# Attention with float32r query and key parts in two row tiles in place of bfloat16 parts in column strips

## What is computed

```
q, k, v = x @ Wq.T, x @ Wk.T, x @ Wv.T        # 32 heads of 16; rope on q and k
scores = q @ k.T / 4 + bias[head, i - j]      # bias only where 0 <= i - j < 256
scores = where(i >= j, scores, -inf)
m = max(max_j scores, offset[head])
p = exp(scores - m); out = p @ v / (sum p + exp(offset - m)); y = out @ Wo.T
```

## Time and profile before

| what | value |
|---|---|
| median of 3 runs | 1722.41 us (1719.87 to 1722.74) |
| the profiled execution | 1717.11 us, span 1714.8 us |
| mean granted clock of PE | 0.949 of 2.4 GHz |
| busy in the span | PE 1549.6, PE weight loads 772.6, DVE 1261.3, ACT 866.5, POOL 226.5 us |
| instructions of PE | 22192 products and as many weight loads |
| stack pieces | 192 DMAs of 128.0 KB for each stack |

### The profile page before, as it was taken

One profiled execution on the slowest core, in us unless ns is written; L12 is line 12 of the kernel. 1 busy time (PEld: TensorE's weight loads), 2 busy tenths in 40 slices (PEclk: granted clock), 3 DMA queues, 4 the chain that ended last, 5 costly groups with the idle time before them and its releaser, 6 DMA issues.

```text
span 1714.8 us, 59791 instructions
## 1 busy us (share of the span) xinstructions
PE 1549.6 (90%) x22192; PEld 772.6 (45%) x22192; DVE 1261.3 (74%) x3801; ACT 866.5 (51%) x1148; POOL 226.5 (13%) x102
## 2 busy tenths in 40 slices
PE   7999999938999998999999899899999999788873
PEld 3444444402554555555545454455455454344331
DVE  2444444468887888888788788788788883489996
ACT  2333333211665665566565566566566668444442
POOL 4333333330000000000000000000000000044543
PEclk9999999955999999999999999999899999999995
DMA  5444444772353353263263255244344402112221
GB/s 212 153 147 147 150 156 164 131 176 36 77 90 62 74 100 54 60 113 62 54 118 64 54 98 81 56 80 79 68 76 80 79 24 95 36 48 88 73 74 49
DMA packets 127099, 155.90 MB, mean 91 GB/s; under 512 B 18240, under 2 KB 82880, under 8 KB 126560
## 3 DMA queue, kind: packets, MB, share of 16 engines
q1 hardware_dynamic: 126816, 152.12, 37.4%
HBM read 100.78 MB, written 50.50 MB: 88 GB/s over the span
## 4 chain that ended last, share of the span: by engine, by line
PE 55%; DVE 20%; issue 18%; POOL 3%; DMA 2%; ACT 1%; DVEq 1%; SPq 0%; POOLq 0%; ACTq 0%
PE ps L636 14%; PE ps L703 10%; PE ps L682 10%; PE ps L662 10%; PE ps L688 6%; DVE junk L1141 6%; DVE mx L1134 4%; PE ps L795 2%; POOL probs L1016 2%; PE ps L713 1%; DVE mx L1141 1%; POOL probs L1052 1%; DVE stats L1317 1%; DMA attn<-wvT 1%; DVE work L1249 1%
## 5 line engine op out<-in xcount | busy, mean ns | idle before, releaser
L881 ACT ACTIVATE probs<-ps 128x1024 f32<-128x1024 f32 (+3 forms) x768 | 604.3, 812 | 375.1 <-PE ps L688 341.3
L1141 DVE CUSTOM_DVE_ANT_0 junk<-ps,bias_q 128x384 bf16<-128x384 f32 (+2 forms) x1024 | 500.3, 502 | 112.4 <-PE ps L662 93.2
L662 PE MATMUL ps<-k_stack,q_stack 96*32 96x384 bf16 (+3 forms) x6144 | 519.4, 341 | 52.5 <-DVE mx L1141 30.2
L682 PE MATMUL ps<-q_stack,k_stack 99*32 99x512 bf16 (+3 forms) x6144 | 514.2, 333 | 9.6 <-issue 7.2
L1134 DVE TENSOR_REDUCE mx<-ps 128x1 f32<-128x128 f32 (+3 forms) x768 | 362.1, 485 | 30.0 <-PE ps L662 25.1
L688 PE MATMUL ps<-toep,flip 96*32 96x384 bf16 (+2 forms) x5120 | 370.8, 284 | 4.5 <-issue 4.4
L636 PE MATMUL ps<-attn 128*128 128x512 f32 x768 | 332.6, 596 | 10.4 <-DMA attn<-hT 9.7
L703 PE MATMUL ps<-probs,v_sb 128*32 128x512 f32 (+3 forms) x3072 | 319.1, 489 | 0.1
L662 PEld LDWEIGHTS ps<-k_stack,q_stack 96*32 96x32 bf16 x6144 | 168.4, 97 | 292.3 <-DVE mx L1141 105.2
L636 PEld LDWEIGHTS ps<-attn 128*128 128x128 f32 x768 | 146.7, 191 | 195.5 <-issue 195.5
L682 PEld LDWEIGHTS ps<-q_stack,k_stack 99*32 99x32 bf16 x6144 | 167.3, 96 | 137.8 <-issue 68.6
(11 more groups left out here) (88 smaller groups left out, 957.3 us busy)
## 6 DMA issues: line engine op xcount, KB each, us to landing
q_stack<-q_parts SPq DMA_DIRECT2D x192, 128.0 KB, 4.0
k_stack<-k_parts SPq DMA_DIRECT2D x192, 128.0 KB, 4.1
v_dram<-v_sb SPq DMA_DIRECT2D x32, 512.0 KB, 2.7
v_sb<-v_dram SPq DMA_DIRECT2D x128, 128.0 KB, 3.8
q_parts<-q_stack SPq DMA_DIRECT2D x96, 128.0 KB, 1.9
k_parts<-k_stack SPq DMA_DIRECT2D x96, 128.0 KB, 2.0
attn<-hT SPq DMA_DIRECT2D x8, 1024.0 KB, 6.2
q_stack<-h SPq DMA_DIRECT2D x16, 512.0 KB, 3.9
```

The lines of the kernel that those rows point to most:

```text
L662: mm = pe.matmul(ps_ring[STRIP * a:STRIP * (a + 1), use.bank, 0:c1 - c0], q_stack[0:STACK, b, hl, i:i + STRIP], k_stack[0:STACK, b, hl, c0 ...
L682: mm = pe.matmul(ps_s[STRIP * a:STRIP * (a + 1), u % 2, hh, 0:w], k_stack[0:ROWS, b, hl, j:j + STRIP], q_stack[0:ROWS, b, hl, i0:i0 + w], ...
L881: act.activation(probs[:, (u // 2) % 3, 2 * pr:2 * pr + 2, 0:w], ps_s[:, pr, :, 0:w], ACT.Exp).then_inc(exp_done, 1)
L1141: ins = dve.tensor_tensor_reduce(out=junk[:, use.bank, 0:c1 - lo], in0=ps_ring[:, use.bank, lo - c0:c1 - c0], in1=bias_q[:, hl, BAND - t0 ...
```

## The change

Query and key are kept in two float32r parts (a 4-byte type that is rounded for PE) instead of three bfloat16 parts. Three pieces of 16 rows make 48, and two shift rows 50. Heads 0 and 1 of the group stand in partitions 0 to 49, heads 2 and 3 in 64 to 113, so two heads' products use two row tiles of 64 rows and all 128 columns of the array. A score unit is two products instead of eight, a maxima unit one instead of four, ordered so that neighbours use different row tiles. The bias of all four heads now follows the second unit of a tile, ahead of PV. The maxima are spread over 24 units. Phase 1 has one ACT copy and one DVE subtraction less for each pair, the shift split two DVE steps less. The store of parts is 4 DMAs of 256 KB for each pair instead of 6 of 128 KB; a stack still has 12 pieces. The ones of slots 2 and 3 come by DMA instead of a memset.

```diff
-STACK = 6 * D
-ROWS = STACK + PARTS
+QK_PARTS = 2
+TERMS = 3
+STACK = TERMS * D
+ROWS = STACK + QK_PARTS
+ROW_TILES = 2
+ROW_TILE = P // ROW_TILES
+PAIR = HG // ROW_TILES
-Q_PART = (0, 0, 0, 1, 1, 2)
-K_PART = (0, 1, 2, 0, 1, 0)
-PIECES = 2 * len(Q_PART)
+Q_PART = (0, 0, 1)
+K_PART = (0, 1, 0)
+PIECES = 2 * TERMS * ROW_TILES
+def max_of(k):
+    pair, rest = divmod(k, NMU * ROW_TILES)
+    unit, e = divmod(rest, ROW_TILES)
+    return e, pair, e * PAIR + pair, unit
-SPREAD = 22
+SPREAD = 24
...
 def load_piece(g, b, buf, i):
-                r = i // 2
+                r, e = divmod(i // 2, ROW_TILES)
-                sp.dma_start(dst[D * r:D * (r + 1), buf, :, :],
-                             src[part[r], :, bass.ds(g * HG, HG), b * S:(b + 1) * S])\
+                p0 = ROW_TILE * e + D * r
+                sp.dma_start(dst[p0:p0 + D, buf, :, :].bitcast(FP32),
+                             src[part[r], :, bass.ds(g * HG + e * PAIR, PAIR), b * S:(b + 1) * S])\
...
-                        if i % 3 == 2 and b == 1 and not last:
-                            hl = i // 3
-                            wait_then_address(ring_read, Use(g, b, (hl + 1) * NMU - 1, last).before + 1)
-                            load_bias_q(g + 1, hl)
+                    for pair in range(PAIR) if b == 1 and not last else ():
+                        wait_then_address(ring_read, Use(g, b, (pair + 1) * NMU * ROW_TILES - 1, last).before + 1)
+                        for e in range(ROW_TILES):
+                            load_bias_q(g + 1, e * PAIR + pair)
...
 def maxima(g, b, ks, use_of):
-                    for a in range(STRIPS):
-                        i = I * P + STRIP * a
-                        mm = pe.matmul(ps_ring[STRIP * a:STRIP * (a + 1), use.bank, 0:c1 - c0],
-                                       q_stack[0:STACK, b, hl, i:i + STRIP], k_stack[0:STACK, b, hl, c0:c1],
-                                       start=True, stop=True)
-                    mm.then_inc(ring_filled, 1)
+                    pe.matmul(ps_ring[:, use.bank, 0:c1 - c0], q_stack[rows, b, a, I * P:(I + 1) * P],
+                              k_stack[rows, b, a, c0:c1], start=True, stop=True).then_inc(ring_filled, 1)
...
+            def scores(g, b, n, u):
+                T, a = divmod(u, PAIR)
+                c, J, i0, w = tile_cols(T)
...
+                pe.wait_ge(exp_done, slot_free(n * NU + u, 2))
+                for e in range(ROW_TILES):
+                    rows = slice(ROW_TILE * e, ROW_TILE * e + ROWS)
+                    mm = pe.matmul(ps_s[:, a, e, 0:w], k_stack[rows, b, a, J * P:(J + 1) * P],
+                                   q_stack[rows, b, a, i0:i0 + w], start=True, stop=not band_cols(T)[1])
+                if not band_cols(T)[1]:
+                    mm.then_inc(scored, 1)
+
+            def biases(g, slot, b, T):
...
+                for pair in range(PAIR) if bw else ():
+                    for e in range(ROW_TILES):
                         for a in range(STRIPS):
                             c0 = b0 + STRIP * (STRIPS - 1 - a)
+                            mm = pe.matmul(ps_s[STRIP * a:STRIP * (a + 1), pair, e, 0:bw], flip[:, :],
+                                           toep[:, slot, e * PAIR + pair, c0:c0 + bw], start=False, stop=True)
+                    mm.then_inc(scored, 1)
...
                     for u in range(NU):
-                        inner, behind = units_beside(u) if more else ((), ())
-                        scores(g, slot, b, n, u, lambda: maxima(ga, ba, inner, use_of))
+                        scores(g, b, n, u)
+                        if more:
+                            maxima(ga, ba, units_beside(u), use_of)
+                        if u % 2:
+                            biases(g, slot, b, u // 2)
                         if b and u == PV_LEFT:
                             pv(g, b - 1, n - 1, NT - 1)
                         if u % 2 and u > 1:
                             pv(g, b, n, u // 2 - 1)
-                        maxima(ga, ba, behind, use_of)
...
-                act.activation(probs[:, (u // 2) % 3, 2 * pr:2 * pr + 2, 0:w], ps_s[:, pr, :, 0:w],
+                act.activation(probs[:, (u // 2) % 3, pr::PAIR, 0:w], ps_s[:, pr, :, 0:w],
...
-            def third_part(b, pair):
-                dve.wait_ge(rot_mid, b * 8 + pair + 1)
-                dve.tensor_tensor(part_bufs[pair % 4][:, 2, :, :], rest, part_bufs[pair % 4][:, 1, :, :],
-                                  ALU.subtract).then_inc(rot_lo, 1)
+            def low_part(b, pair):
+                dve.wait_ge(rot_hi, b * 8 + pair + 1)
+                dve.tensor_tensor(part_bufs[pair % 4][:, 1, :, :], rot[:, pair % 2, :, :],
+                                  part_bufs[pair % 4][:, 0, :, :].bitcast(FP32), ALU.subtract).then_inc(rot_lo, 1)
```

More of the change, by code:

```diff
@@ L128, in ring_order @@
             if more:
-                order += [(b, k) for ks in units_beside(u) for k in ks]
+                order += [(b, k) for k in units_beside(u)]
             if b and u == MT_LEFT and not (last and b > B - AHEAD):
@@ L281, in build @@
         ps_o = ps[:, 7, :]
-        st3 = [q_stack[:, i, :, :].rearrange("p a t -> p (a t)").bitcast(FP32) for i in range(4)] + \
-              [k_stack[:, i, :, :].rearrange("p a t -> p (a t)").bitcast(FP32) for i in range(4)]
+        st3 = [late[:, i, :] for i in range(8)]
         def wide(i, half):
@@ L523, in phase1 @@
                         wait_then_address(rot_lo, b * 8 + pair + 1)
-                        for s in range(PARTS):
+                        for s in range(QK_PARTS):
                             for a in range(2):
@@ L545, in _ @@
             load_stack(0, 2, 2)
+            for e in range(ROW_TILES):
+                ones = slice(ROW_TILE * e + STACK, ROW_TILE * e + ROWS)
+                for buf in (2, 3):
+                    sp.dma_start(k_stack[ones, buf, :, :].bitcast(FP32), k_stack[ones, 0, :, :].bitcast(FP32)).then_inc(ones_copied, 16)
             sp.wait_ge(ext_parts_stored, 16)
             load_toep(0, slice(0, 1))
-            load_shift(0, 0)
-            load_shift(1, 1)
+            load_shift(Use.first(0, NM), 0)
+            load_shift(Use.first(1, NM), 1)
             def phase2(g, last):
@@ L653, in maxima @@
                 for k in ks:
-                    I, c0, c1 = MAX_UNITS[k % NMU]
-                    hl = k // NMU
+                    e, a, hl, unit = max_of(k)
+                    I, c0, c1 = MAX_UNITS[unit]
+                    rows = slice(ROW_TILE * e, ROW_TILE * e + STACK)
                     if k == 0:
@@ L686, in scores @@
+            def biases(g, slot, b, T):
+                b0, bw = band_cols(T)
+                if T == 0 and b == 0:
+                    pe.wait_ge(toep_loaded, 16 * PARTS * (g + 1))
+                for pair in range(PAIR) if bw else ():
+                    for e in range(ROW_TILES):
                         for a in range(STRIPS):
                             c0 = b0 + STRIP * (STRIPS - 1 - a)
-                            mm = pe.matmul(ps_s[STRIP * a:STRIP * (a + 1), u % 2, hh, 0:bw], flip[:, :],
-                                           toep[:, slot, hl, c0:c0 + bw], start=False, stop=True)
@@ L994, in _ @@
             pool.wait_ge(ident_ready, 2)
-            pool.memset(k_stack[STACK:ROWS, 0:2, :, :], 1.0).then_inc(ones_set, 1)
-            pool.wait_ge(ones_set, 1)
+            for e in range(ROW_TILES):
+                rows = slice(ROW_TILE * e + 2 * D, ROW_TILE * (e + 1))
+                pool.memset(k_stack[rows, 0:2, :, :].bitcast(FP32), 1.0).then_inc(ones_set, 1)
+            pool.wait_ge(ones_set, 2)
             for r in range(2):
@@ L1033, in _ @@
             pool.wait_ge(rot_lo, 32)
-            for i in range(4):
-                pool.wait_ge(parts_stored[i], FIRST + 16 * 6 * 8)
-            pool.memset(k_stack[STACK:ROWS, 2:4, :, :], 1.0).then_inc(ones_set, 1)
-            pool.wait_ge(ones_set, 4)
             pool.wait_ge(ring_read, ALL_USES)
@@ L1129, in max_unit @@
                 dve.wait_ge(ring_filled, use.before + 1)
[L1130 removed]
+                if unit == 0:
                     dve.wait_ge(bias_q_loaded[hl], 16 * (g + 1))
@@ L1290, in phase2 @@
                     for u in range(NU):
-                        inner, behind = units_beside(u) if more else ((), ())
-                        for ks in (inner, behind):
-                            for k in ks:
-                                max_unit(ga, k, ba % 2, use_of(k))
+                        for k in units_beside(u) if more else ():
+                            max_unit(ga, k, ba % 2, use_of(k))
                         if b and u == MT_LEFT and not (last and b > B - AHEAD):
```

115 lines of the change are left out of this document (44 added, 71 removed).

## The result

| | before | after |
|---|---|---|
| median | 1721.14 us (1717.52 to 1722.74, 4 runs) | 2133.99 us (2108.74 to 2173.35, 4 runs) |
| profiled execution, span | 1717.11, 1714.8 us | 2108.74, 2106.8 us |
| mean granted clock | 0.949 | 0.804 |

The ratio is 1.231 (95% interval 1.221 to 1.240); it takes of the four runs after only the two fastest (2109 and 2127 us), since the others lie more than 1.5% above the fastest, while the medians stand for all four. By the medians the change costs 413 us; the direction was forecast, the size was not (1835, at most 1905). The page of the profile after: busy times, the granted clock in 40 slices of 52.7 us, and the groups of ACT's exponentials, the maxima, DVE's reading of them, and the scores.

What follows compares the result with a forecast made beforehand. The prediction took the loop as bound by hand-overs between PE, DVE and ACT: +4.5 x 30 = +135, -6, -16 on 1717.1 gives 1830, and with 5.3 for the median 1835 us; range 1690 to 1905.

Steps and rivals of the forecast that it cites:

- rival (d): Attention loop: PE's clock falls to 1.2 GHz in a quarter of the passes, +110, giving 1945 us; chance 0.06.
- the walk: One loop pass, tile by tile, durations put in order of issue: 31.3 us before, 35.8 after.
- The pass at full rate: Attention loop: a pass grows from 31.3 to 35.8 us, +4.5 in each of 30 passes, +135 us.
- Float32r: Score and maxima products: 512 columns stream in 0.22 us, as in bf16; a weight load takes 0.11, 0.06 exposed.
- rival (c): Score and maxima products: float32r streams at half rate, 40.0 us a pass, giving 1961 us; chance 0.06.
- Rival (b): Score and maxima products: row tiles don't run side by side, 37.0 us a pass, giving 1871 us; chance 0.08.
- Switches: PE between row tiles and bias or PV strips: 0.15 us each way, 24 a pass, 1.9 us of the growth.
- ACT's wait for the bias line: Attention loop, a sign of being right: ACT waits longer for the bias line than 317 us.
- Rival (a): Attention loop: hand-overs overlap more, DVE sets a pass of 28 us, giving 1602 us; faster has chance 0.17.
- End of phase 1: End of phase 1, from 350.51 to 367.6 us: one ACT copy and two DVE subtractions go, -6 us.
- Issue gaps: PE's loop: a quarter off the 62.2 us of score loads waiting for nothing visible, -16 us; ends zero and 50.
- PE busy under 75%: Attention loop, a sign of being right: PE's busy share falls under 75% while DVE's falls too.

Runs made afterwards that it cites:

- e4: Kernel before (bfloat16 parts) with the bias of all heads after the second unit, maxima behind the scores and spread over 24 units; 1838.57 us.
- e6: Kernel after, but the bias of each pair of heads follows that pair's scores and maxima, as before the change; 1834.11 us.
- e9: Kernel after, with DVE forming the shift behind the maxima of the next pass's second unit, except at turns between groups of heads; 2037.77 us.
- e1: Kernel after with each score and maxima product issued twice into the same place; 2110.56 us.
- e10: Kernel after with both the bias order of e6 and the moved shift of e9; 1836.23 us.
- e8: Kernel before with only its maxima spread over 24 units instead of 22; 1753.04 us.
- e3: Kernel after with only its maxima spread over 22 units, as before the change; 2077.73 us.
- e2: Kernel after with only the maxima products issued twice; 2143.99 us.

## Why the prediction was wrong

**The step that failed is rival (d), the clock**, and the forecast's own sum, which kept every duration at 2.4 GHz. I had a reason in hand (PE streams 22 of 36 us, and rows 1 show 1.2 GHz in the DVE-bound slices), priced it "in a quarter of the passes" at +110 and gave it 0.06. In the trace it is in all of the 30 passes but the first: 40% of their tiles lie at 1.2 GHz for more than half of their length, for +216 us. The price for all of it was in the text, "over 50 us a pass"; the share was a guess from no row. What the rows could have said: the two slices at 0.5 in rows 1 are stretches in which PE waits for DVE again and again, and the walk showed the same kind of wait in the first tile of each pass. That would have named the risk and not its size. The loss is no term that either half of the change brings alone: above the full-rate pass the kernel before loses 1.8 us, the new order with the old parts 1.9 (e4), the new parts with the bias behind each unit 2.8 (e6), both together 9.0.

**Point by point, the rest of the sum.**

- *The pass at full rate:* 35.8 forecast, about 37.0 measured. The last tile 2.6 forecast, 2.68 measured; the tile with the first full band 3.7 and 3.7; the first tile 3.6 forecast, 4.0 measured, of which the shift's chain makes more than the walk had (3.2 in e9, where it is moved). The walk wasn't exact for the kernel before either: its sum of 31.3 us is right, but its second tile, 3.3, is 2.8 in the trace. e4 shows that 3.7 of the 5.7 us are the order's, with the old parts.
- *Float32r:* 0.22 us for 512 columns was right. The maxima follow the scores of 512 columns after 0.34 us (915.93 to 916.27), those of 256 after 0.22 (910.30 to 910.52): 0.11 more for 256 more columns, one column a cycle, and 0.11 of load ahead of them, of which I had taken 0.06. So rival (c) is out.
- *Row tiles side by side:* the two products of a pair start 4 ns apart (grouped as x2 above). Rival (b) is out.
- *Switches:* 0.15 us each way forecast, 0.10 measured: PV of 384 columns from 912.51 streams 0.64 (three quarters of 0.86), to 913.15, and the scores start at 913.26. The other way, the maxima at 911.69 last 0.44 us, less the latency of 0.17 to 911.96, and the bias starts at 912.06. The Trainium skill (TensorEngine Tiling (Array Packing), Key Properties) says that a change of tiling mode drains TensorE; the 0.10 agrees with a short drain. It is a small price: e6 pays it twice as often and is 300 us faster.
- *ACT's wait for the bias line:* it grew as foretold, from 323.4 us (430 to 1400) to 719.1 (430 to 1800); a part of that is the clock's.
- *Rival (a), faster through DVE:* never near. DVE's share in the loop is 60% (828 of 1370 us); it waits for PE.
- *End of phase 1:* -6 forecast, -2.7 measured. *Issue gaps:* -16 forecast; the score loads still wait 53.3 us for nothing visible (62.2 before), so it was about -9 at most, and the bias's loads now have 86.3 us of such waits where they had 10.2, in 375 short pieces; these stand at the switches.
- *"PE busy under 75%"* failed as a test: at 1.2 GHz products last twice as long and the record shows 92% (1254.65 of 1370). *"A clock below 0.9 in the loop"*, named there as what would refute me, is what came.

With the clock's share put right (+216) and the full-rate pass at 37.0, the same sum gives 1717 + 171 + 216 + 6 = 2110, the profiled execution. That closes the books by measured terms and is no second forecast.

## What to carry to other kernels

A change that takes streams out of PE while the loop stays bound by hand-overs does not leave PE's clock alone: here 8 us fewer of streams in a pass of 31 cost 216 us through the clock once the bias came late, and only 30 (2.8 less 1.8 us in 30 passes) where it stayed behind each unit. Before forecasting, list PE's stops after the change, price the products behind each at both levels, and give the low level a wide range, since no run here tells which stops count; then look for the stop that can be moved (the shift's chain: -96 us) or for the order that has fewer (bias behind each unit: -300 us). Work that is issued once instead of twice to save switches (0.10 us each) is a bad trade when ACT waits for its result.

## What was not expected of the hardware

- Adding products cost nothing or even won time: e1 issues twice the score and maxima products and takes 2111 us against 2134; 2 us of unread strips a group took e10 from 1836 to 1811.
- After a stop of about 1 us (0.96 at the turn; 1.3, 0.8 and then up to 3.3 around the group's) the clock stood at 1.2 GHz for up to 44 us, although PE's record shows it busy 39.85 of 40 us in one such stretch. The Trainium skill (TensorE: Matmul & The Clock Gate, Part 1) says that the level follows how busy PE has recently been; the falls agree, the long stay in a stretch that looks full does not follow from the busy record.
- Stops of 1.3 to 1.8 us at six turns in e8 brought one fall of 3.4 us, where 0.7 to 1.0 us in the kernel after had a fall behind it each time. What makes a stop count, together with the streams around it, no run here settles: e3 has fewer streams per time than e2 and the same clock (0.84 and 0.85), with shorter and more numerous falls.
- The time of the kernel after scatters by 3% (2109 to 2173 us), where before scatters by 0.3% in the runs of the first table and by 0.9% at most in later ones. That small shifts at a turn decide whole stretches of 40 us would fit, but isn't shown.
